# A gated convolution pair on one core: edge rows of eight images as blocks, seven-slot blocks for the first two pairs, and two engines' work ordered by round

## The reference

```
def qconv_cg(x, w, theta):           # base = 64 // 4 = 16 channels
    yp = conv3x3(x[:, :base], w[:, :base])
    yr = conv3x3(x[:, base:], w[:, base:])
    d = sigmoid(2.0 * (yp - theta))
    return yp + d * yr
h = relu(bn(qconv_cg(x, w_a, theta_a), gamma_a, beta_a, mean_a, var_a))
h = bn(qconv_cg(h, w_b, theta_b), gamma_b, beta_b, mean_b, var_b)
return relu(x + h)
```

## Time and profile before

| | us |
|---|---|
| median of three runs | 453.05 |
| profiled execution, its own time | 452.76 |
| its span, first to last instruction | 450.9 |
| outside the span | 1.9 |
| PE busy / DVE busy / ACT busy / POOL busy | 439.8 / 245.7 / 209.4 / 7.5 |

### The profile page before, as it was taken

One profiled execution on the slowest core, in us unless ns is written; L12 is line 12 of the kernel. 1 busy time (PEld: TensorE's weight loads), 2 busy tenths in 40 slices (PEclk: granted clock), 3 DMA queues, 4 the chain that ended last, 5 costly groups with the idle time before them and its releaser, 6 DMA issues.

```text
span 450.9 us, 16900 instructions
## 1 busy us (share of the span) xinstructions
PE 439.8 (98%) x7829; PEld 434.3 (96%) x7829; DVE 245.7 (54%) x407; ACT 209.4 (46%) x336; POOL 7.5 (2%) x23
## 2 busy tenths in 40 slices
PE   8999999999999999999999999999999999999992
PEld 7999999999999999999999999999999999999991
DVE  5566466437536644653754565465456536534634
ACT  6386355345345345443543543464355435424322
POOL 6000000000000000000000000000000000000000
PEclk9999999999999999999999999999999999999997
DMA  9940000073407160250808061060603030003116
GB/s 173 197 89 2 4 3 1 15 132 67 80 3 145 26 122 4 58 89 1 145 3 144 4 120 27 3 132 16 135 12 72 4 73 5 1 3 73 38 38 143
DMA packets 116421, 27.06 MB, mean 60 GB/s; under 512 B 116224, under 2 KB 116224, under 8 KB 116352
## 3 DMA queue, kind: packets, MB, share of 16 engines
q1 hardware_dynamic: 115440, 25.86, 30.9%
q10 hardware_dynamic: 592, 0.13, 0.1%
q0 software_dynamic: 320, 0.00, 0.1%
HBM read 13.14 MB, written 12.85 MB: 58 GB/s over the span
## 4 chain that ended last, share of the span: by engine, by line
PE 94%; DMA 2%; DVE 2%; ACT 1%; issue 1%; DVEq 0%; ACTq 0%
PE acc L398 94%; DMA out_dram<-rows_out 1%; DMA x<-in_x_dram 1%; DVE mix L654 1%; DVE mix L652 1%; DVE rows_out L669 0%; ACT L523 0%; PE acc L429 0%; PE acc L346 0%; ACT rows_out L542 0%; ACT mix L523 0%; ACT x_hi L491 0%; ACT w_hi L475 0%; DVE x L569 0%; DVEq L651 0%
## 5 line engine op out<-in xcount | busy, mean ns | idle before, releaser
L398 PE MATMUL acc<-h_hi,w_hi 32*128 32x512 f32 (+1 forms) x1248 | 269.7, 389 | 0.0
L398 PE MATMUL acc<-h_lo,w_hi 32*128 32x512 f32 (+1 forms) x1248 | 268.7, 389 | 0.0
L398 PE MATMUL acc<-h_hi,w_lo 32*128 32x512 f32 (+1 forms) x1248 | 267.4, 387 | 0.0
L398 PE MATMUL acc<-x_hi,w_hi 32*128 32x456 f32 x1344 | 263.9, 366 | 0.6 <-DVE mix L654 0.5
L398 PE MATMUL acc<-x_hi,w_lo 32*128 32x456 f32 x1344 | 264.1, 366 | 0.0
L398 PE MATMUL acc<-x_lo,w_hi 32*128 32x456 f32 x1344 | 264.0, 365 | 0.0
L398 PEld LDWEIGHTS acc<-x_hi,w_hi 32*128 32x128 f32 x1344 | 214.3, 183 | 2.5 <-DVE mix L654 1.3
L398 PEld LDWEIGHTS acc<-x_lo,w_hi 32*128 32x128 f32 x1344 | 215.9, 183 | 0.3
L398 PEld LDWEIGHTS acc<-x_hi,w_lo 32*128 32x128 f32 x1344 | 214.9, 183 | 0.4
L398 PEld LDWEIGHTS acc<-h_lo,w_hi 32*128 32x128 f32 x1248 | 200.8, 183 | 0.2
L398 PEld LDWEIGHTS acc<-h_hi,w_lo 32*128 32x128 f32 x1248 | 200.7, 183 | 0.1
(11 more groups left out here) (57 smaller groups left out, 41.3 us busy)
## 6 DMA issues: line engine op xcount, KB each, us to landing
out_dram<-rows_out SPq DMA_DIRECT2D x30, 392.0 KB, 6.4
x<-in_x_dram SPq DMA_DIRECT2D x28, 392.0 KB, 5.4
x<-in_x_dram SPq DMA_DIRECT2D x2, 280.0 KB, 4.2
x<-in_x_dram SPq DMA_DIRECT2D x2, 266.0 KB, 4.9
out_dram<-rows_out SPq DMA_DIRECT2D x4, 126.0 KB, 2.5
x<-in_x_dram SPq DMA_DIRECT2D x2, 112.0 KB, 4.3
w_nat<-in_L_conv_w_a_dram SPq DMA_DIRECT2D x1, 144.0 KB, 3.0
w_nat<-in_L_conv_w_b_dram SPq DMA_DIRECT2D x1, 144.0 KB, 3.9
```

Source lines behind the costliest of these rows:

```text
L398: return pe.matmul(sums(bank, blk), w[g * ROWS:(g + 1) * ROWS, tap], moving(blk, part, c, dx, g), start=(u == 0 and (alone or g == FIRST_G ...
```

## The change

- **Second convolution.** h's ring keeps 28 slots an image and no shared or shifted slots. Each image has three b blocks of nine slots (slots 1 to 27), 48 in all. The two edge rows of each image (the first and the last) go into two new "e" blocks: eight images each, a slot per image, 8 slots = 456 columns, with weight tiles of their own (`w_edge_hi`, `w_edge_lo`) and inputs `e_hi`, `e_lo`, which GpSimd (POOL) copies from `h_hi` and `h_lo` (52 copies of one or two rows). Their x comes by DMAs of its own into `x_edge`, which shares memory with the early weight tiles. 50 blocks of the second convolution instead of 52.
- **First convolution.** The first two pairs of images are cut in blocks of seven slots (399 columns less one: 398), eight blocks a pair; the other six pairs stay at seven blocks of 456. 16 + 42 = 58 blocks instead of 56. The chunks of x that are split follow the blocks; the first loads of x are a slot shorter.
- **Order by round.** ACT and DVE do first the three leading blocks' gates and sums, then what leaves blocks r0 and r1, then block r3's gate and sums, then what leaves r2 and r3, and all splits of x last. AHEAD is 8 instead of 6.
- **Output.** `rows_out` is a ring of four blocks; each block is stored by itself with two DMAs of up to 126 KB.
- **Start.** The second weights' transposes stand at steps 40 and 50; the parts around the batch norm are reordered. Filler matmuls have 398 columns. The last five second blocks are b45, b46, b44, b47, e1.

```
 BLK, BLK_B = 8, 9
+SHORT, SHORT_PAIRS = 7, 2
-AHEAD, SOON = 6, 4
+W_BANK, W_STEPS = 4, (40, 50)
+AHEAD, SOON = 8, 4
...
-    b_blocks = [(ring * HRING + t, min(BLK_B, HRING - t))
-                for ring in range(B // H_IMGS) for t in range(0, HRING, BLK_B)]
+    a_slots = []
+    for pair in range(B // 2):
+        size = SHORT if pair < SHORT_PAIRS else BLK
+        for img in (2 * pair, 2 * pair + 1):
+            a_slots += [[(img, t, size)] for t in range(0, SLOTS - size + 1, size)]
+        if SLOTS % size:
+            a_slots.append([(2 * pair, SLOTS - HALF, HALF), (2 * pair + 1, SLOTS - HALF, HALF)])
...
+    second = []
+    for img in range(B):
+        second += [("b", 3 * img + r) for r in range(3)]
+        if img == EDGE:
+            second.append(("e", 0))
+    second[-4:] = [second[-3], second[-2], second[-4], second[-1], ("e", 1)]
```

On GpSimd, the copies of edge rows:

```
+            for n in edge_sources:
+                img, s, k = a_slots[n][0]
+                if img == EDGE and s == 0:
+                    for g in range(GROUPS):
+                        pool.wait_ge(visit_done[g], visits(g, place["e", 0]))
+                pair = len(a_slots[n])
+                for tile, h, ready in ((e_hi, h_hi, hhi_ready), (e_lo, h_lo, hlo_ready)):
+                    pool.wait_ge(ready, n + 1)
+                    at, to = (SLOTS - 1, tile[:, 0]) if s else (0, tile[:, 1])
+                    src = slots(h, (img % H_IMGS) * SLOTS, pair * SLOTS).rearrange("p (i s) w -> p i s w", i=pair)
+                    nc.gpsimd.tensor_copy(slots(to, img % EDGE, pair), src[:, :, at]).then_inc(edges_ready, 1)
```

On TensorE, the second weights' steps and, in `moving`, an e block's input:

```
-                if step in (46, 60):
+                if step in W_STEPS:
...
+                if kind == "e":
+                    return (e_hi, e_lo)[part][rows, c, dx:dx + EDGE * PITCH]
```

On ScalarE, the order of a round:

```
-            for b in range(0, TOTAL, ROUND):
-                gate(b)
-                split_ahead(b)
-                gate(b + 1)
-                split_ahead(b + 1)
-                finish(b)
-                gate(b + 2)
-                finish(b + 1)
-                finish(b + 2)
-                split_ahead(b + 2)
-                gate(b + 3)
-                finish(b + 3)
-                split_ahead(b + 3)
+            for first in range(0, TOTAL, ROUND):
+                for b in range(first, first + 3):
+                    gate(b)
+                for b in range(first, first + 2):
+                    finish(b)
+                gate(first + 3)
+                for b in range(first + 2, first + 4):
+                    finish(b)
+                for b in range(first, first + 4):
+                    split_ahead(b)
```

On VectorE, the order of a round:

```
-            for b in range(0, TOTAL, ROUND):
-                split_ahead(b)
-                mix_sums(b)
-                split_ahead(b + 1)
-                mix_sums(b + 1)
-                low_parts(b)
-                mix_sums(b + 2)
-                low_parts(b + 1)
-                low_parts(b + 2)
-                split_ahead(b + 2)
-                mix_sums(b + 3)
-                low_parts(b + 3)
-                split_ahead(b + 3)
+            for first in range(0, TOTAL, ROUND):
+                for b in range(first, first + 3):
+                    gated(b)
+                    summed(b)
+                for b in range(first, first + 2):
+                    leave(b)
+                gated(first + 3)
+                summed(first + 3)
+                for b in range(first + 2, first + 4):
+                    leave(b)
+                for b in range(first, first + 4):
+                    split_ahead(b)
```

On SyncE, loads and stores:

```
+            sp.wait_ge(wt_ready, 4)
+            load_x_edge(0)
+            for m, (kind, n) in enumerate(second):
+                if kind == "b" and n % 3 == 0 and 0 < n and n // 3 - 1 + X_IMGS < B:
+                    img = n // 3 - 1
+                    sp.wait_ge(resid_ready, residual_done(img))
+                    load_x(sp, img + X_IMGS, 0, XS, x_landed[img % X_IMGS])
...
+                store(m)
```

More of the change, by code:

```diff
@@ L66, in a_of @@
[L66 to L84, removed]
@@ L86, in b_done @@
-    def b_done(img, slot=XS):
-        return sum(t < XS * img + slot for t, k in b_blocks)
+    HRING = H_IMGS * SLOTS
+    EDGE = BLK
+    assert BLK_B * PITCH - 1 <= BANK and SLOTS == 3 * BLK + HALF == 3 * BLK_B + 1 and B % EDGE == 0
+    a_slots = []
[4 more added lines that the diff above has]
+        if SLOTS % size:
+            assert SLOTS % size == HALF
+            a_slots.append([(2 * pair, SLOTS - HALF, HALF), (2 * pair + 1, SLOTS - HALF, HALF)])
@@ new lines, in gated_conv_pair_kernel, with b_slots, a_needed @@
+    NA = len(a_slots)
+    a_of = {(img, t): n for n, parts in enumerate(a_slots) for img, first, k in parts
+            for t in range(first, first + k)}
+    NB, NE = 3 * B, B // EDGE
+    second = []
[4 more added lines that the diff above has]
+    second[-4:] = [second[-3], second[-2], second[-4], second[-1], ("e", 1)]
+    def b_slots(n):
+        return n // 3, 1 + n % 3 * BLK_B, BLK_B
+    def a_needed(blk):
+        kind, n = blk
+        if kind == "e":
+            return a_of[(n + 1) * EDGE - 1, SLOTS - 1] + 1
+        img, s0, k = b_slots(n)
+        return max(a_of[img, t] for t in range(s0 - 1, s0 + k)) + 1
@@ L91, in gated_conv_pair_kernel @@
     order, place = [], {}
-    for n in range(NA + NB):
+    for n in range(NA + len(second)):
         na = sum(kind == "a" for kind, m in order)
         nb = len(order) - na
-        ready = nb < NB and na >= a_needed(nb) and place["a", a_needed(nb) - 1] + MARGIN <= n
-        blk = ("b", nb) if na == NA or ready and order[-1][0] == "a" else ("a", na)
+        ready = nb < len(second) and na >= a_needed(second[nb]) and place["a", a_needed(second[nb]) - 1] + MARGIN <= n
+        blk = second[nb] if na == NA or ready and order[-1][0] == "a" else ("a", na)
@@ L206, in gated_conv_pair_kernel @@
         out_ready = sem("out_ready")
-        out_stored = [sem(f"out_stored{n}") for n in range(OUT_IMGS)]
+        out_stored = [sem(f"out_stored{n}") for n in range(OUT_RING)]
+        wedge_zero = sem("wedge_zero")
+        wedge_ready = sem("wedge_ready")
+        ecols_zero = sem("ecols_zero")
+        edges_ready = sem("edges_ready")
+        x_edge_landed = [sem(f"x_edge_landed{n}") for n in range(NE)]
         def slots(tile, t, k):
@@ L314, in _ @@
+            for n in range(OUT_RING):
+                sp.wait_ge(out_stored[n], 32 * len(range(n, len(second), OUT_RING)))
         @block.gpsimd
```

326 lines of the change are left out of this document (183 added, 143 removed).

## The result

The changed kernel takes 442.39 us (median of 4 runs, 441.99 to 442.68) against 452.99 for the kernel before in the same comparison: 0.9767, 95% interval 0.975 to 0.9784. The sign was right, the size was not. The profiled execution took 441.99.

A forecast was written before the change was run, and what follows sets the result against it. PE's streamed columns were taken to bound the kernel: 2.6 us from the start, 5.66 from columns, 0 from rounds, less 0.8 at the end, net -7.5 from 453.05, stated as 445.4 us; range 443.7 to 449.5.

The forecast's parts named there:

- e1: An edge block, last of the second convolution: its store was forecast held behind r2's until T + 5.5, 0.8 us later.
- What bounds the kernel: Whole kernel: the columns PE streams set the time, then start and end; 2.4 us in 417 lost to small waits.
- Columns: Group 0's 105 blocks: 754 fewer columns per unit, 5.66 us gained if short units take 0.1843 us.
- Start: Up to group 0's restart at 25.12: 1.8 us from shorter steps plus 0.8 from waits, restart at 22.5.
- The rounds: VectorE's two operations on r0 before group 0's r3: margin 0.3 to 0.4 us; net change 0, bounds -0.4 and +2.
- The load: Image 11's load, issued in the round that splits its first chunk: could delay r0 by up to 0.5 us once.
- The end: After the last matmul: r2's store holds e1's in SyncE's queue; costs 0.8 us, bounds 0 and 1.5.
- T: The end of the last matmul, 441.97 in the kernel before, forecast at 433.7 after.
- A: Rival: PE cannot issue short units' load and matmul pairs that fast; 3.6 us lost, 449; chance 0.09 (447 to 449.5).
- B: Rival: units of 398 columns cost what 456 do everywhere, so no net gain, 453.0; chance 0.04.
- C: Rival: VectorE late to r0 every round, 453.5 to 463, chance 0.06; weak form, some rounds, 447 to 449.5, chance 0.09.
- GpSimd: Its 52 edge copies and four of 192 columns: all hidden, unless a copy of about 0.35 us holds VectorE.

The follow-up runs named there:

- places alone: Kernel before with MARGIN 9 instead of 8, so b blocks stand at r1 and r3 in nearly all rounds: 452.14 us against 452.94 (0.9979).
- the order with splits last: Kernel before with splits of x at the round's end, residuals right behind their sums, AHEAD 8; r0's h_lo and ScalarE's order also moved: 452.22 against 453.03 (0.9978).
- Residuals alone: Changed kernel with the b blocks' residuals put back right behind their sums, splits last as in the change: 440.63 us (0.9726).
- splits alone: Changed kernel with only the splits of x put back where they were, on both engines, AHEAD 8: 451.99 us (0.9973).

## Why the prediction was wrong

*What bounds the kernel*: right, PE by its columns, 0.184, 0.208 and 0.232 us a unit. The clause "there is little to win by scheduling" is where it failed. I had the 2.4 us of loss in the sum and then went by the earlier trace rows, which list two waits. The rest are pieces of 0.1 to 0.3 us in which no load begins while matmuls are in flight, seen only in the starts.

*Columns*: 5.66, confirmed by the traces; alone, without shorter work for VectorE, they would be worth 5.5 us in time together with the start's steps. *Start*: 2.6 against 2.9; the wait for r0's sums went as worked out, but with nothing to spare where 0.25 was reckoned: the sums end at 22.19, group 0 begins at 22.23, and the other groups' starts go on at 0.18.

*The rounds*, "Both together: 0", with at most 0.4 to gain: the first step that failed, measured 1.6. I counted that VectorE has 3.6 us free a round, but the place where that time lies matters: r0 as a b block takes 0.13 more of a margin of 0.3, and a split of 0.7 to 0.9 ahead of r1's sums comes on top. The runs show both parts: on the kernel before, places alone took 0.8 off the loss, the order with splits last 1.4; together they can't add up, for there were 1.6 to win. Residuals alone had no share. That the split by itself is what counted in that order is argued, not shown: on the kernel after, splits alone cost nothing without a late load.

*The load* that I named as "one place is closer", at most 0.5, never showed in the change; but with AHEAD 8 it costs 8 to 10 us if the splits aren't last. That I priced the wait without the queue behind it was wrong by far.

*The end*, "+0.8", measured -0.6: the second step that failed; the path was right, its sizes were not. 0.6 of the 1.4 is that r3's sigmoid starts at T + 0.2 and not at T + 0.8, with all behind it. ScalarE comes to it sooner because VectorE is done sooner: that engine begins at T - 5.8 and not at T - 5.57, and operations that don't depend on each other follow at 0.60 to 0.63 and not at the 0.71 of dependent ones. VectorE's first sums of the last round, its two residuals, and SyncE's last issues:

```profile
426.03 0.68 DVE L745 TENSOR_TENSOR mix<-mix,acc 128x504 f32<-128x504 f32 x1 [6.91 <-PE acc L486]
426.75 0.68 DVE L749 TENSOR_TENSOR mix<-mix,acc 128x504 f32<-128x504 f32 x1
427.35 0.68 DVE L745 TENSOR_TENSOR mix<-mix,acc 128x504 f32<-128x504 f32 x1
...
430.00 1.39 DVE L764 SCALAR_TENSOR_TENSOR rows_out<-mix,inv,x 128x504 f32<-128x504 f32 x2
...
436.73 1.34 SPq L336 DMA_DIRECT2D out_dram<-rows_out  x2
```

The second sum waits for the first (0.72 from start to start), the third for neither of them (0.60). Eight operations take 5.36 us, 0.67 each, and are done at 431.39 and not at T + 0.1 = 431.93. The rest of the 1.4 is the last landing, 2.3 us from issue instead of 2.7 (0.4), and a shorter end behind it (0.4); why these are shorter no run shows. That r2's store holds e1's was right: e1's ReLU ends at 435.93 and its store is issued 0.8 later. With r2 first in the last round 0.2 of that is left, with the residuals between the sums nothing.

*Rivals*: A, B and C are out for the change; C in a few rounds is what the old splits did with AHEAD 8. *GpSimd*: by the Trainium skill, "SBUF — State Buffer", "Who interferes with whom", its reads and VectorE's operations on two SBUF inputs exclude each other. The trace agrees: the same copy takes 0.23 beside a sum, which has one input in PSUM, and 0.63 when it meets an `h_lo` of 0.57, and it is GpSimd that is held.

```profile
23.69 0.23 POOL L421 CAST e_hi<-h_hi 128x57 fp32r<-128x57 f32 x1 [1.58 <-ACT h_hi L633]
...
28.94 0.57 DVE L772 TENSOR_TENSOR h_lo<-mix,h_hi 128x392 fp32r<-128x392 f32 x1 [0.78 <-ACT h_hi L633]
28.97 0.63 POOL L421 CAST e_hi<-h_hi 128x57 fp32r<-128x57 f32 x1 [3.56 <-ACT h_hi L633]
```

What stays open: how the loss that the change removed divides between places and order, which part of the order it is, and why the first unit begins 6.9 to 7.7 us into the span from run to run.

## What to carry to other kernels

Compare the bound engine's time with the sum of its own work; what is over is waiting, even where the waits list none, if several streams share the engine. Put work that nobody waits for soon (splits ahead) behind all work with a thin margin, above all work that can itself wait for a load. At the end of a program fill an engine's wait with the residual that frees the store queue.

## What the runs showed of the hardware

Loads and matmuls of four row groups still followed at 0.13 us a group for 284 columns, 0.033 us a pair. After 2.6 us in which no matmul ran, the granted clock was 0.50 (1.2 of 2.4 GHz) for 3.4 us: two units of 456 columns of one group began 0.38 us apart instead of 0.21. After 2.8 us without a matmul, 30 us later in the same run, it stayed at 1.00.
